# Normalised rows by one ScalarE operation of scale and bias, and a new step order on every engine

## The chip, the core and the metric

The kernel runs on one core of a Trainium2 chip. The core has a matrix engine (TensorE, PE; its weight loads are listed apart as PEld), a vector engine (VectorE, DVE), an activation engine (ScalarE, ACT), a general engine (GpSimd, POOL) and SyncE (SP), which here only issues DMAs. Each engine runs its own instruction list in order, and the lists meet only at semaphores. The metric is the device time of one execution in microseconds, the median of three.

## What is computed

One block of a transformer with adaptive layer norm over x of 8 batches x 1024 rows x 256 features, in fp32. The weights are 256x1024 and 1024x256.

```
h = layernorm(x) * (1 + ca) + sa              # ca, sa, ga, cb, sb, gb: one row of 256 per batch
x = x + ga * softmax((h*w_lhs) @ (h*w_rhs)^T) @ h
h = layernorm(x) * (1 + cb) + sb
x = x + gb * (relu(h @ W1 + b1) @ W2 + b2)
```

A layer norm is (x - mean) / sqrt(var + eps) over the 256 features of a row. Where products need more than the fast matmul format holds, an operand is split into a rounded part (`hi`) and a rest (`lo`), and three matmuls stand for one.

## The kernel before

Rows lie in tiles of 128 partitions, so a batch has 8 tiles in two halves (HT = 4). The work of a batch is cut into steps, and for each engine a table of text gives the order of the steps (`FIRST_STEPS` for batch 0, `SECOND_STEPS` for batch 1, `STEPS` for a loop over batches 2 to 6, `LAST_STEPS` for batch 7, `AFTER_STEPS` behind it). A suffix `-` means the step belongs to the batch before, `+` to the one after. So attention of batch b runs between the two feed-forward layers of batch b-1. `part` of each engine walks its table and emits the code of each step. Nothing else sets the order.

The steps that matter here, with n the tile or half:

- SC.n (PE: scores of a tile; DVE L864: copy to S with row maximum), ST and MX (DVE: stage blocks of S, row maxima of the lower half), MB.n (PE L655: maxima turned to columns), SB.n (DVE L887/L892: subtract the maximum), EX.n (ACT L793: exp), SM.n (ACT L806 rounded part `Phi`, DVE L911 rest `Plo`), AV.n (PE L690 to L694: attention times values; DVE L917 to L932: scale, add to x, statistics of the new row).
- L1.n: statistics of the next batch's rows (DVE L951/L954), and on POOL, in `statistics` (L1065), nm = -mean, var + eps and rs = 1/sqrt(var + eps). L2.n: the same for the rows behind attention.
- N1.n and N2.n: four row tiles of `ln_t` normalised as (x + nm) * rs, in `normalise` (L1074 to L1080) on POOL. Behind them stand BH.n and B2.n (DVE L990/L991: 32x32 transposes), a store and a load that complete the transpose (SP: SH/RH, S2/R2), and TH.n and T2.n (ACT and DVE: features scaled, shifted and split).
- VN.n (ACT L783): x + nm to `ln_v`, four tiles; VL.n (DVE L1038): times rs and the modulation row, four tiles; V.n (ACT L788, DVE L980): split into V.
- F.n (PE L593 to L595: a block of the first layer, six matmuls; ACT L715 relu and L719 rounded part; POOL L1088 the rest `hid_lo`), G.n (PE L530 to L536: second layer, twelve matmuls), OUT.n (DVE L1026/L1030: result times gb plus x), GT and OT (the last tiles), TP.0 (PE L662: transposes of batch 0's rows on PE).
- XG.n (DVE L1051), XC.n (POOL L1139): additions to x.

PE waits for: `scores_read`, `av_read`, `v_done` (V.n is split), `plo_done`, `hid_hi_done`, `hid_lo_done`, `col_read`, and at G.8 for `out_done`, since the accumulator of G.0 to G.7 must have been read by OUT.0.

Of the kernel before, what the change touches and what calls it, by code (L numbers as in the profile page):

```python
# [1170 lines left out]
```

## Time and profile before

| what | value |
|---|---|
| time, three executions | 693.47, 693.54, 694.78 us; median 693.54 us |
| profiled execution, first to last instruction (span) | 691.5 us |
| busy: PE, weight loads, DVE, ACT, POOL | 686.1, 627.7, 558.4, 427.5, 361.7 us |
| granted TensorE clock, mean | 1.00 of full speed |
| DMA: moved, mean rate | 77.54 MB, 112 GB/s |

The profile is one execution. It gives its span and no other time of its own: the median lies 2.0 us above the span, which is what lies around the first and the last instruction. Busy times of different engines overlap, so they don't add up to the span.

### The profile page before, as it was taken

Reading aid. Unit: us, or ns where it says so; the run is one execution under the profiler, and the core shown is the slowest. Engines: PE = TensorE matmul, PEld = TensorE weight load, DVE = VectorE, ACT = ScalarE, POOL = GpSimd, SP = SyncE. Lnnn points to the kernel's source line nnn. Section 1 sums busy time; section 2 is a strip of 40 time slices with the busy share of each in tenths; the row PEclk is TensorE's granted clock in tenths of the full one; section 3 lists DMA queues with packets and bytes.
Section 4 is the critical chain, followed back from the end, with each engine's and each line's share of the span. In section 5 each row is a group of like instructions: output and inputs, shape, how many; then the busy total and the mean of one; then the engine's idle time right before and its main releaser. Section 6 shows DMA issues by size and latency. Waiting matters only on the chain.

```text
span 691.5 us, 13488 instructions
## 1 busy us (share of the span) xinstructions
PE 686.1 (99%) x4621; PEld 627.7 (91%) x4621; DVE 558.4 (81%) x1059; ACT 427.5 (62%) x625; POOL 361.7 (52%) x396
## 2 busy tenths in 40 slices
PE   9999999999999999999999999999999999999998
PEld 8688899998999989998999989999899998999997
DVE  5699989799898898978989799887989887876421
ACT  3265398736786367683786647864678634845562
POOL 3572576636654386352872458643665434523644
PEclk9999999999999999999999999999999999999999
DMA  8211761137431382315622266112843126003300
GB/s 294 81 49 59 204 193 55 39 107 252 123 100 56 103 232 91 99 61 179 180 67 90 67 226 185 61 38 98 258 121 99 46 91 221 1 1 100 100 31 30
DMA packets 61663, 77.54 MB, mean 112 GB/s; under 512 B 5632, under 2 KB 54336, under 8 KB 61632
## 3 DMA queue, kind: packets, MB, share of 16 engines
q1 hardware_dynamic: 61632, 77.14, 35.5%
q8 instruction: 18, 0.29, 0.2%
q14 instruction: 13, 0.11, 0.1%
HBM read 46.15 MB, written 30.97 MB: 112 GB/s over the span
## 4 chain that ended last, share of the span: by engine, by line
PE 94%; DVE 4%; issue 0%; ACT 0%; DMA 0%; DVEq 0%; ACTq 0%; SPq 0%
PE col L595 9%; PE col L594 9%; PE col L593 9%; PE acc L530 8%; PE acc L531 8%; PE acc L536 8%; PE score L694 8%; PE score L690 8%; PE score L691 8%; PE score L578 4%; PE score L579 4%; PE score L580 4%; PE score L576 2%; PE score L584 2%; PE score L499 1%; DVE S L879 1%
## 5 line engine op out<-in xcount | busy, mean ns | idle before, releaser
L1088 POOL TENSOR_TENSOR hid_lo<-hid,hid_hi 128x512 fp32r<-128x512 f32 x127 | 175.4, 1386 | 143.2 <-ACT hid_hi L719 142.8
L715 ACT ACTIVATE hid<-col,b1T 128x512 f32<-128x512 f32 x128 | 87.0, 679 | 140.3 <-PE col L595 126.1
L530 PE MATMUL acc<-W2hi,hid_hi 128*128 128x256 f32 x480 | 119.2, 282 | 0.0
L531 PE MATMUL acc<-W2lo,hid_hi 128*128 128x256 f32 x480 | 116.9, 278 | 0.0
L690 PE MATMUL score<-V,Phi 128*128 128x258 f32 x448 | 108.8, 281 | 0.0
L691 PE MATMUL score<-V,Phi 128*128 128x256 f32 x448 | 108.6, 281 | 0.0
L719 ACT ACTIVATE hid_hi<-hid 128x512 fp32r<-128x512 f32 x128 | 81.0, 633 | 37.6 <-PE acc L536 29.8
L593 PE MATMUL col<-h2hi,W1hi 128*128 128x512 f32 x256 | 102.4, 400 | 0.0
L595 PE MATMUL col<-h2hi,W1lo 128*128 128x512 f32 x256 | 101.0, 395 | 0.0
L594 PE MATMUL col<-h2lo,W1hi 128*128 128x512 f32 x256 | 100.6, 393 | 0.0
L530 PEld LDWEIGHTS acc<-W2hi,hid_hi 128*128 128x128 f32 x480 | 90.4, 188 | 2.1
L531 PEld LDWEIGHTS acc<-W2lo,hid_hi 128*128 128x128 f32 x480 | 90.2, 188 | 1.8
L690 PEld LDWEIGHTS score<-V,Phi 128*128 128x128 f32 x448 | 85.0, 190 | 0.7
L691 PEld LDWEIGHTS score<-V,Phi 128*128 128x128 f32 x448 | 84.0, 188 | 0.6
L1069 POOL TENSOR_SCALAR nm<-mv 128x4 f32<-128x4 f32 x32 | 16.7, 523 | 129.2 <-DVE mv L932 104.2
L911 DVE TENSOR_TENSOR Plo<-S,Phi 128x1024 fp32r<-128x1024 f32 x56 | 70.2, 1269 | 8.1 <-ACT Phi L806 6.4
L536 PE MATMUL acc<-W2hi,hid_lo 128*128 128x256 f32 x480 | 76.6, 276 | 0.0
L864 DVE TENSOR_SCALAR_CACHE_REDUCE S<-score 128x1024 f32<-128x1024 f32 (+1 forms) x64 | 62.7, 980 | 15.2 <-PE score L584 12.9
L793 ACT ACTIVATE S<-S 128x1024 f32<-128x1024 f32 (+1 forms) x64 | 64.4, 1019 | 13.2 <-DVE S L879 7.7
L1139 POOL TENSOR_TENSOR x_cur<-x_cur,attn_mod 128x512 f32<-128x512 f32 x32 | 43.3, 1354 | 40.8 <-DVE ln_v L1038 40.8
L536 PEld LDWEIGHTS acc<-W2hi,hid_lo 128*128 128x128 f32 x480 | 64.6, 188 | 0.0
L694 PE MATMUL score<-V,Plo 128*128 128x258 f32 x448 | 62.8, 282 | 0.0
(139 smaller groups left out, 1493.2 us busy)
## 6 DMA issues: line engine op xcount, KB each, us to landing
block_rows<-blocks SPq DMA_DIRECT2D x29, 512.0 KB, 2.9
blocks<-block_rows SPq DMA_DIRECT2D x116, 128.0 KB, 3.0
x_cur<-x SPq DMA_DIRECT2D x16, 512.0 KB, 3.9
ln_t<-x SPq DMA_DIRECT2D x14, 512.0 KB, 4.8
score_blocks<-stage SPq DMA_DIRECT2D x14, 512.0 KB, 4.2
lower<-score_blocks SPq DMA_DIRECT2D x56, 128.0 KB, 2.9
out<-x_mlp SPq DMA_DIRECT2D x8, 512.0 KB, 3.0
out<-x_mlp SPq DMA_DIRECT2D x15, 256.0 KB, 2.2
```

What stands on the lines that cost most here:

```text
L530: nc.tensor.matmul(o, hi, W2hi[:, it, :], start=(it == 0 and (apart or t % 2 == 0)), stop=False, skip_group_check=True)
L531: nc.tensor.matmul(o, hi, W2lo[:, it, :], start=False, stop=False, skip_group_check=True)
L536: last = nc.tensor.matmul(o, lo, W2hi[:, it, :], start=False, stop=(it == FT - 1), skip_group_check=True)
L593: nc.tensor.matmul(col[n % 2][:], W1hi[:, kk, tile], h2hi[:, kk, cols], start=(kk == 0), stop=False)
L594: nc.tensor.matmul(col[n % 2][:], W1hi[:, kk, tile], h2lo[:, kk, cols], start=False, stop=False)
L595: last = nc.tensor.matmul(col[n % 2][:], W1lo[:, kk, tile], h2hi[:, kk, cols], start=False, stop=(kk == DK - 1))
L690: nc.tensor.matmul(o, Phi[:, slot, t, :], V[:, t, 0:VW], start=(t == 0), stop=False)
L691: nc.tensor.matmul(o[:, 0:D], Phi[:, slot, t, :], V[:, t, VP:VP + D], start=False, stop=False)
L694: last = nc.tensor.matmul(o, Plo[:, slot, t, :], V[:, t, VP:VP + VW], start=False, stop=(t == T - 1))
L715: nc.scalar.activation(hid[:, n % 2, :], col[n % 2][:], ACT.Relu, bias=b1T[:, n % FT:n % FT + 1]).then_inc(col_read, 1)
L719: nc.scalar.activation(hid_hi[:, n % RING, :], hid[:, n % 2, :], ACT.Copy).then_inc(hid_hi_done, 1)
L1088: G.tensor_tensor(hid_lo[:, n % RING, :], hid[:, n % 2, :], hid_hi[:, n % RING, :].bitcast(F32), ALU.subtract).then_inc(hid_lo_done, 1)
```

## The change

`normalise` on POOL is gone. N1 and N2 are steps of ACT now, each four activations that compute x * rs + nb, where nb = nm * rs is a new small operation at the end of `statistics` (with one more semaphore, `ln1_power` or `ln2_power`, between). VN computes x * rs + nb as well, so `ln_v` holds normalised rows, and VL on DVE is one tensor-tensor product with the modulation row over all four tiles, in place of four operations of two products. All tables of steps are new.

```diff
-        SC.6 SC.7 BH.0+ SB.2 VL.1 SM.0 MX.0 SB.3 V.1 L1.1+ SM.1 SB.4 OUT.0- AV.0 BH.1+ SB.5 AV.1 SM.2 SM.3
+        SC.7 BH.0+ VL.1 SB.1 SM.0 MX.0 SB.2 SB.3 L1.1+ OUT.0- SB.4 V.1 SM.1 SB.5 SM.2 BH.1+ AV.0 AV.1 AV.2
...
-                            nc.scalar.activation(ln_v[:, t, :], x_cur[:, i, :], ACT.Identity, bias=nm1[:, i:i + 1]).then_inc(v_mean, 1)
+                            nc.scalar.activation(ln_v[:, t, :], x_cur[:, i, :], ACT.Identity, scale=rs1[:, i:i + 1], bias=nb1[:, i:i + 1]).then_inc(v_mean, 1)
...
+                    elif kind == "N1":
+                        act.wait_ge(ln1_rstd, 2 * b + 3 + n)
+                        for t in range(HT):
+                            i = n * HT + t
+                            last = nc.scalar.activation(ln_t[:, t, :], ln_t[:, t, :], ACT.Identity, scale=rs1[:, i:i + 1], bias=nb1[:, i:i + 1])
+                        last.then_inc(ln1_done, 1)
+                    elif kind == "N2":
...
+                        act.wait_ge(ln2_rstd, 2 * batch + n + 1)
+                        for t in range(HT):
+                            i = n * HT + t
+                            last = nc.scalar.activation(ln_t[:, t, :], x_cur[:, i, :], ACT.Identity, scale=rs2[:, i:i + 1], bias=nb2[:, i:i + 1])
+                        last.then_inc(ln2_done, 1)
...
-                        for t in range(HT):
-                            i = n * HT + t
-                            dve.wait_ge(v_mean, HT * (2 * b + n - 2) + t + 1)
-                            V_.scalar_tensor_tensor(ln_v[:, t, :], ln_v[:, t, :], rs1[:, i:i + 1], attn_mod[:, 0, :], ALU.mult, ALU.mult).then_inc(v_ln, 1)
+                        dve.wait_ge(v_mean, HT * (2 * b + n - 2) + HT)
+                        V_.tensor_tensor(ln_v[:], ln_v[:], attn_mod[:, 0:1, :].broadcast_to([P, HT, D]), ALU.mult).then_inc(v_ln, HT)
...
-                G.tensor_tensor(rs[:, tiles], var_eps[:], half_power[:], ALU.pow).then_inc(rstd_done, 1)
-
-            def normalise(out_tiles, in_tiles, nm, rs, h, rstd_done, count, done):
-
-                wait_apart(pool, rstd_done, count)
-                for t in range(HT):
-                    i = h * HT + t
-                    last = G.tensor_scalar(out_tiles[:, t, :], in_tiles[:, t, :], nm[:, i:i + 1], rs[:, i:i + 1], ALU.add, ALU.mult)
-                last.then_inc(done, 1)
+                G.tensor_tensor(rs[:, tiles], var_eps[:], half_power[:], ALU.pow).then_inc(power_done, 1)
+                pool.wait_ge(power_done, count)
+                G.tensor_tensor(nb[:, tiles], nm[:, tiles], rs[:, tiles], ALU.mult).then_inc(rstd_done, 1)
```

Where the steps moved, at three places. DVE in the loop over batches 2 to 6, before: SB.3 (L889/L892) is followed by V.1 (L980) and the statistics of the next rows (L951).

```order
283 L903 TENSOR_TENSOR row_max<-row_max,left_max 128x4
284 L889 TENSOR_TENSOR S<-S,score 128x4x128
285 L892 TENSOR_TENSOR S<-lower,score 128x4x128
286 L980 TENSOR_TENSOR V<-ln_v,V 128x4x256
287 L364 ISA
288 L948 REGISTER_ALU
289 L951 BN_STATS stats<-ln_t 128x6 x4
```

The same engine and place of the change, from the first product of OUT.0 (L1050, L1054) on.

```order
292 L1054 TENSOR_TENSOR x_mlp<-acc,x_mlp 128x512
293 L1049 ISA
294 L1050 TENSOR_TENSOR acc<-acc,gb_all 128x512
295 L1053 REGISTER_ALU
296 L1054 TENSOR_TENSOR x_mlp<-acc,x_mlp 128x512
297 L911 TENSOR_TENSOR S<-S,score 128x8x128
298 L1004 TENSOR_TENSOR V<-ln_v,V 128x4x256
```

V.1 (L1004) now stands behind OUT.0 and SB.4 (L911), which waits for MB.1 of PE. On PE, MB.1 is followed by F.12, G.10 and AV.0 now; before, G.7 and then AV.0 followed it.

ACT in the same loop of the change: N1.1 (L815) and V.1 (L792) between F.10 (L719/L723) and EX.3 (L797).

```order
178 L719 ACTIVATE hid<-col,b1T 128x512
179 L720 REGISTER_ALU
180 L723 ACTIVATE hid_hi<-hid 128x512
181 L812 REGISTER_ALU
182 L815 ACTIVATE ln_t<-ln_t,nb,rs 128x256 x4
183 L790 REGISTER_ALU
184 L792 ACTIVATE V<-ln_v 128x4x256
185 L796 REGISTER_ALU
186 L797 ACTIVATE S<-S 128x8x128
```

ACT in that place before: V.1 (L788) came earlier, between F.8 and F.9 (L715/L719).

```order
160 L715 ACTIVATE hid<-col,b1T 128x512
161 L716 REGISTER_ALU
162 L719 ACTIVATE hid_hi<-hid 128x512
163 L786 REGISTER_ALU
164 L788 ACTIVATE V<-ln_v 128x4x256
165 L715 ACTIVATE hid<-col,b1T 128x512
```

So four activations came in, in front of a V.1 that itself stands two F steps later.

POOL at the end of the program, before: the last L2.1 (L1069 to L1072) and N2.1 (L1079) stand ahead of the last feed-forward blocks.

```order
146 L1069 TENSOR_SCALAR nm<-mv 128x4
147 L1070 TENSOR_SCALAR var_eps<-mv 128x4
148 L1072 TENSOR_TENSOR rs<-var_eps,half_power 128x4
149 L1079 TENSOR_SCALAR ln_t<-x_cur,nm,rs 128x256 x4
150 L1088 TENSOR_TENSOR hid_lo<-hid,hid_hi 128x512 x15
```

The same of the change.

```order
143 L1091 TENSOR_SCALAR nm<-mv 128x4
144 L1092 TENSOR_SCALAR var_eps<-mv 128x4
145 L1094 TENSOR_TENSOR rs<-var_eps,half_power 128x4
146 L1096 TENSOR_TENSOR nb<-nm,rs 128x4
147 L1104 TENSOR_TENSOR hid_lo<-hid,hid_hi 128x512 x15
```

N2.1 has left POOL; on ACT it stands behind the first two F steps of `AFTER_STEPS`. The AV.7 of batch 7, on whose rows it works, was followed by G.12, F.15 and G.13 to G.15 on PE and is now PE's last step of batch 7.

## Rows read from the trace of the kernel before

**Rows 1.** The page: engine shares, and the shares of the chain that ended last.

```profile
PE 686.1 (99%) x4621; PEld 627.7 (91%) x4621; DVE 558.4 (81%) x1059; ACT 427.5 (62%) x625; POOL 361.7 (52%) x396
...
PE 94%; DVE 4%; issue 0%; ACT 0%; DMA 0%; DVEq 0%; ACTq 0%; SPq 0%
```

**Rows 2.** Busy us by stage: window, its us, PE, PEld, DVE, ACT, POOL, clock, DMA.

```profile
0.00:17.39 17.39, 15.81 (x112) 14.50 (x113) 8.86 (x31) 5.35 (x10) 5.85 (x16) 1.00 0.87 295
17.39:67.64 50.25, 49.92 (x231) 38.52 (x232) 42.96 (x103) 23.37 (x32) 26.58 (x33) 1.00 0.20 64
67.64:150.61 82.97, 82.85 (x571) 76.44 (x571) 73.41 (x139) 54.81 (x81) 47.15 (x48) 1.00 0.41 121
...
315.08:397.32 82.24, 82.24 (x572) 76.36 (x571) 71.52 (x132) 54.68 (x80) 44.63 (x48) 1.00 0.38 121
...
644.01:688.13 44.12, 44.10 (x290) 39.97 (x288) 12.97 (x18) 23.62 (x36) 23.71 (x23) 1.00 0.16 51
688.13:691.50 3.37, 0.00 (x0) 0.00 (x0) 0.85 (x2) 0.00 (x0) 0.59 (x1) 0.98 0.46 156
```

**Rows 3.** The waits of PE: total us, times, longest.

```profile
PE score L683 <- DVE x_cur L926: 0.3, 1, 0.3
```

**Rows 4.** Groups of instructions: line, engine, shapes, count | busy us, mean ns.

```profile
L1079 POOL TENSOR_SCALAR ln_t<-x_cur,nm,rs 128x256 f32<-128x256 f32 x64 | 37.8, 606 | 3.4 <-POOL rs L1072 2.3 <-issue 1.0
L1072 POOL TENSOR_TENSOR rs<-var_eps,half_power 128x4 f32<-128x4 f32 x32 | 35.6, 1112 | 2.7
L1079 POOL TENSOR_SCALAR ln_t<-ln_t,nm,rs 128x256 f32<-128x256 f32 x56 | 31.4, 577 | 1.5 <-POOL rs L1072 1.5
L1038 DVE SCALAR_TENSOR_TENSOR ln_v<-ln_v,rs,attn_mod 128x256 f32<-128x256 f32 x56 | 24.5, 498 | 0.5 <-ACT ln_v L783 0.4
L736 ACT ACTIVATE featT<-blocks,mod_b 128x512 f32<-128x512 f32 x30 | 24.2, 807 | 16.0 <-DMA blocks<-block_rows 11.2 <-DVE Rlo L999 4.8
L783 ACT ACTIVATE ln_v<-x_cur,nm 128x256 f32<-128x256 f32 x56 | 23.7, 495 | 0.7 <-DMA x_cur<-x 0.7
L745 ACT ACTIVATE h2hi<-featT 128x512 fp32r<-128x512 f32 x32 | 20.2, 633 | 1.0
L1070 POOL TENSOR_SCALAR var_eps<-mv 128x4 f32<-128x4 f32 x32 | 9.5, 297 | 2.2
```

**Rows 5.** In time order: batch 7's G.7 and two F steps, and OUT.0 on DVE.

```profile
667.33 0.28 PE L530 MATMUL acc<-W2hi,hid_hi 128*128 128x256 f32 x1
...
668.34 0.70 DVE L1026 TENSOR_TENSOR acc<-acc,gb_all 128x512 f32<-128x512 f32 x1 [7.53 <-PE acc L536]
...
668.72 0.39 PE L593 MATMUL col<-h2hi,W1hi 128*128 128x512 f32 x1
...
670.09 0.39 PE L593 MATMUL col<-h2hi,W1hi 128*128 128x512 f32 x1
...
670.40 0.69 DVE L1030 TENSOR_TENSOR x_mlp<-acc,x_mlp 128x512 f32<-128x512 f32 x1
```

**Rows 6.** Batch 7's MB.1 and SB.4 in time order, and the line of V.n.

```profile
604.30 0.60 PE L655 MATMUL score<-ident,row_max 128*128 128x128 f32 x4
...
604.93 1.22 DVE L887 TENSOR_TENSOR S<-S,score 128x1024 f32<-128x1024 f32 x1 [1.00 <-PE score L655]
...
L980 DVE TENSOR_TENSOR V<-ln_v,V x14: 1211/1474/1660, 84.4 to 598.9; 128x1024 fp32r<-128x1024 f32 x14
```

**Rows 7.** Batch 0: TP.0 on PE, and the read of AV.7 on DVE.

```profile
63.07 1.04 PE L662 MATMUL score<-ident,ln_t 128*128 128x128 f32 x8
...
68.91 0.42 DVE L926 TENSOR_TENSOR x_cur<-score,x_cur 128x256 f32<-128x256 f32 x1
```

**Rows 8.** The last rows' chain: N2.1 (POOL), T2.1 (ACT, DVE).

```profile
644.55 2.18 POOL L1079 TENSOR_SCALAR ln_t<-x_cur,nm,rs 128x256 f32<-128x256 f32 x4 [0.21 <-issue]
...
657.24 0.80 ACT L736 ACTIVATE featT<-blocks,mod_b 128x512 f32<-128x512 f32 x1
...
660.11 0.69 DVE L1002 TENSOR_TENSOR h2lo<-featT,h2hi 128x512 fp32r<-128x512 f32 x1 [0.68 <-ACT h2hi L745]
```

More of the change, by code:

```diff
@@ L80 @@
+        N2.0 TH.1+ EX.7 F.14- SM.7 F.15- T2.0
     """,
     "dve": """
-        SC.0 ST.0 SC.1 B2.1- XG.2- XG.3- SC.2 ST.1 VL.0 ST.2 L1.0+ V.0 SC.3 ST.3 VL.1 SC.4 SB.0 BH.0+ SB.1
-        SB.2 SC.5 T2.1- V.1 SC.6 L1.1+ SC.7 SM.0 MX.0 SM.1 SB.3 AV.0 OUT.0- SB.4 BH.1+ SM.2 AV.1 SB.5 SB.6
-        SM.3 AV.2 AV.3 SM.4 SB.7 XG.0 TH.0+ SM.5 B2.0 XG.1 AV.4 SM.6 AV.5 SM.7 AV.6 TH.1+ AV.7 T2.0 OUT.1-
+        SC.0 ST.0 B2.1- XG.2- SC.1 XG.3- SC.2 ST.1 VL.0 ST.2 V.0 SC.3 ST.3 L1.0+ VL.1 SC.4 SB.0 SC.5 SB.1
@@ L85 @@
+        BH.0+ V.1 T2.1- SC.6 SB.2 SC.7 SM.0 SB.3 MX.0 L1.1+ SB.4 OUT.0- SM.1 SB.5 AV.0 SM.2 BH.1+ AV.1 SM.3
+        SB.6 AV.2 SM.4 TH.0+ AV.3 SB.7 SM.5 XG.0 XG.1 SM.6 AV.4 AV.5 B2.0 TH.1+ AV.6 SM.7 AV.7 OUT.1- T2.0
     """,
     "pool": """
-        N2.1- F.0- XC.0 F.1- F.2- L1.0+ N1.0+ F.3- XC.1 F.4- F.5- F.6- F.7- L1.1+ XC.2 N1.1+ F.8- F.9- XC.3
-        F.10- F.11- F.12- L2.0 N2.0 F.13- F.14- F.15- L2.1
+        F.0- XC.0 F.1- F.2- F.3- L1.0+ F.4- XC.1 XC.2 F.5- F.6- F.7- XC.3 F.8- L1.1+ F.9- F.10- F.11- F.12-
@@ L806, in part @@
                         nc.scalar.activation(Phi[:, n % RING, :, :], S[:, :, n * P:(n + 1) * P], ACT.Copy).then_inc(phi_done, 1)
+                    elif kind == "N1":
[5 more added lines that the diff above has]
+                    elif kind == "N2":
+                        batch = b if n == 0 else f
+                        if n == 1:
+                            act.wait_ge(blocks_done, ph.turn_base(b))
+                        elif "next" in ph.has:
+                            act.wait_ge(blocks_done, ph.turn(b, "TH", 1) + 1)
+                        else:
+                            act.wait_ge(blocks_done, ph.turn(b, "T2", 1) + 1)
+                        act.wait_ge(ln2_rstd, 2 * batch + n + 1)
[3 more added lines that the diff above has]
+                        last.then_inc(ln2_done, 1)
             over_batches(act, part)
@@ L1117, in part @@
                             last.then_inc(w_ready, 1)
-                    elif kind == "N1":
-                        normalise(ln_t, ln_t, nm1, rs1, n, ln1_rstd, 2 * b + 3 + n, ln1_done)
-                    elif kind == "N2":
-                        batch = b if n == 0 else f
-                        if n == 1:
-                            pool.wait_ge(blocks_done, ph.turn_base(b))
-                        elif "next" in ph.has:
-                            pool.wait_ge(blocks_done, ph.turn(b, "TH", 1) + 1)
-                        else:
-                            pool.wait_ge(blocks_done, ph.turn(b, "T2", 1) + 1)
-                        normalise(ln_t, x_cur[:, n * HT:(n + 1) * HT, :], nm2, rs2, n, ln2_rstd, 2 * batch + n + 1, ln2_done)
                     elif kind == "XC":
```

98 lines of the change are left out of this document (51 added, 47 removed).

## The prediction, made before the changed kernel had run

> **What bounds the kernel now.** I read the engine shares first, then the stretches, then the waits of PE. PE is busy 686.1 of 691.5 us, and 94% of the chain that ended last is PE's [rows 1]. A busy share alone may hide short waits, so the stretches decide: batches 2 to 6 take 82.24 us each and PE is busy for all of it [rows 2]. What PE leaves idle is before its work starts (17.39 - 15.81 = 1.6 us), behind its last matmul (3.37 us) and in batches 0 and 1: 0.33 us in the first, and 0.73 us by which the second is longer than a middle one [rows 2]. PE has one wait of 0.3 us in its list [rows 3]. So the reader should see a kernel in which any change of ACT, DVE or POOL is worth nothing unless it makes PE wait, or takes away one of these small remainders. PE's matmuls are the same ones in the change, in another order.
>
> By the Trainium skill (Perfetto Trace Analysis, "Identifying the Most-Contended Engine"), matmul busy time is a bad measure and the busy share of weight loads a good one. That share is 76.36 of 82.24 us in a middle batch [rows 2], so by that rule up to 5.9 us a batch would be open to a better order, 41 us over the five, and the time about 652 us.
>
> I don't follow it: two starts of an F step (six matmuls of 512 columns) lie 670.09 - 668.72 = 1.37 us apart [rows 5], 0.23 us a matmul, in stretches where nothing is waited for, so loads idle there by the length of the matmul and an order can't change that.
>
> **The change part by part.**
>
> *Work taken and added.* POOL loses 120 tile operations, 37.8 + 31.4 = 69.2 us [rows 4], and gains 32 small ones, nb. The trace has none of that kind; between 0.30 (L1070, same width, one input) and 1.11 us (L1072, two inputs, a power) [rows 4] I take 0.3, so 10 us. POOL comes to about 302 us of 691. None of this is on PE's path.
>
> ACT gains the same 120 tiles, 16 a middle batch. An activation with no operand by row takes 633 ns and one with both scale and bias by row 807 ns, at 512 elements [rows 4]: 174 ns for two. VN has one and takes 495 ns at 256 elements [rows 4]. With the second it lies between 495 and 495 + 174 = 669 ns; I take 582, half of the 174 for each. A middle batch gets 16 x 0.582 + 8 x 0.087 = 10.0 us more, so ACT has 64.7 us of 82.24 where it had 54.7 [rows 2]. It fits, if it stands in the right places.
>
> DVE loses four operations of 498 ns in each VL, 2.0 us, and gets one of 1024 elements. Nearest are V.n's 1211 to 1660 ns [rows 6], so it gains 0.3 to 0.8 us a half. DVE is busy 71.5 of 82.24 us [rows 2] and PE doesn't wait for it: nothing.
>
> *Middle batches, G.8.* With the new PE order G.7, F.10, F.11, G.8, the wait for `out_done` comes close. From G.7's first matmul at 667.33 OUT.0 starts after 1.01 us (668.34, when half of G.7 is done) and ends at 670.40 + 0.69 = 671.09, 3.76 us after G.7 began [rows 5]. G.8 begins one G and two F later: 1.39 + 2 x 1.37 = 4.13 us [rows 5]. So 0.37 us are left if DVE is free when G.7's first half is done, and it costs nothing; before, two AV steps stood in between as well. Hidden by: F.10 and F.11.
>
> *Middle batches, AV.0.* On DVE V.1 now waits behind SB.4, which waits for MB.1, and AV.0 of PE waits for V.1. SB.4 starts 0.63 us after MB.1 (604.93 against 604.30) and takes 1.22 us; V.1 takes 1.21 to 1.66 us [rows 6]. So V.1 ends 3.06 to 3.51 us after MB.1 began. AV.0 comes behind MB.1 (an estimate: it shows 0.60 us until its last transpose has drained, and some 0.25 us of that overlap the next step; that is 0.35 us), F.12 and G.10: 0.35 + 1.37 + 1.39 = 3.11 us [rows 5, 6]. The stall is 0 to 0.4 us in each of five batches. I take V.1 at its shortest, since POOL, whose subtractions it can meet, has nothing to do there: F.10's rest is done by then, and F.11's comes after TH.0. Sum 0.0, bound 5 x 0.4 = 2.0 us. On ACT N1.1 (4 x 0.58 = 2.3 us) now stands in front of V.1, behind F.10. F.10 is released 3 x 1.37 = 4.1 us ahead of MB.1 (F.11, G.8 and G.9 stand between) and DVE gets to V.1 1.85 us after MB.1, so ACT has 4.1 + 1.85 = 5.9 us for F.10 (two activations, 1.3), N1.1 (2.3) and V.1 (1024 elements, at most twice the 633 ns: 1.3) [rows 4]: hidden with 1.0 us to spare.
>
> *Batch 0 into 1.* TP.0 (at 63.07, about 0.9 of its 1.04 us until the next matmul) moves behind AV.7, so the read of AV.7, which let the second half of batch 1's SC.0 go on at 68.91 + 0.42 = 69.33 [rows 7], gets that much cover. But TH.1 on DVE, for which SC.0's first half waits, now stands behind AV.6's read. Bounds: the whole 0.73 us by which batch 1 is longer won [rows 2], or 0.4 us lost, one operation of the read (0.42) [rows 7]. I take 0.1 lost, since a read is more than one such operation, and so longer than the cover. The small operation nb also delays batch 0's first normalisation by 0.3 us, but PE's transposes of these rows come after modulation matmuls, and in the second half DVE is still busy with the first: nothing.
>
> *Behind batch 7.* AV.7 is PE's last step of batch 7, so L2.1 and N2.1 start later. N2.1 began at 644.55, 0.54 us after the stretch began, and T2.1's last split ended at 660.11 + 0.69 = 660.80, 16.8 us into it [rows 8]. Now N2.1 stands behind F.1 on ACT: two F on PE (2.74), two activations of 0.63 [rows 4, 5], so from 4.0 on, and 4 x 0.58 us later, at 6.3, it is done, where it was done at 2.7 (644.55 + 2.18). L2.1 with nb (0.3 + 0.3 + 1.1 + 0.3 = 2.0 us [rows 4]) is ready by then if AV.7's read took under 2 us. T2.1's end moves by 0 to 3.6 us, to 16.8 to 20.4: on ACT it began at 657.24 with no idle time ahead of it [rows 8], so it waited for ACT and not for its load, and takes only a part of the delay; I take two thirds, 19.2. F.8 begins after F.0 to F.7 and G.0 to G.5, fourteen steps of 1.37 us, at 19.2. A race with no margin: 0 to 1.2 us. I take 0.
>
> *The sum* against the profiled span: 691.5 + 0.1 = 691.6 us; with the 2.0 us by which the median lay above it, 693.6 us.
>
> **The rivals.**
>
> *DVE comes late to OUT.0 or V.1 (slower).* DVE has 71.5 us of work in 82.24, and its order has waits for PE in it, behind which the rest of the list queues. From 0.37 us of lateness at OUT.0 on, G.8 stalls PE, and from a V.1 over 1.3 us on, AV.0 does. For it: both margins are smaller than anything that PE met before, where it waited once. Against: DVE loses 0.6 to 1.6 us of work a batch ahead of that place. At 0.4 us in each of six batches: 693.6 + 2.4 = 696.0 us. Chance 0.16.
>
> *A lock between POOL and DVE.* V.1 takes 1.21 us or up to 1.66 [rows 6], so something shares a path with it. If a POOL subtraction began just before V.1, and V.1 then waited for all of it, V.1 would end a whole 1.3 us late: five times 1.2 us, 699.6 us. That is the rule of the Trainium skill (SBUF — State Buffer, "SBUF: two separate sides"), by which the pair of ports that DVE and GpSimd share is held for a whole instruction. The 0.45 us between V.n's shortest and longest show a part of it at most. Chance 0.03.
>
> *ACT falls behind (slower).* The new activations take not 0.58 but over 0.83 us each, or meet a wait, and N1.1 uses up the 1.0 us in front of V.1. At 669 ns, the upper bound, it is 0.35 us and nothing happens. With 1.4 us of slip: 0.4 x 5 = 2.0, 695.6 us. Chance 0.03.
>
> *The remainders go (faster).* The 0.33 and 0.73 us of batches 0 and 1 and a part of the 1.6 us at the start: 693.5 - 1.5 = 692.0 us. Chance 0.05. That weight loads tell the truth and the new order packs PE closer gets 0.01.
>
> *It doesn't do what it says*: the normalisation doesn't get shorter at all (577 and 606 ns on POOL, some 582 on ACT). That seems likely to me, and gives the forecast's time.
>
> **How the numbers follow.** Forecast 0.72, with its own range 692.8 to 694.6. The range for 8 in 10 reaches into the remainders' case below and past 696.0 above: 692.4 to 696.5. About 0.2%, 1.4 us, is what a measurement of this kernel can tell from no change. Faster by more needs the remainders or the packing: 0.06. Slower by more: 0.16 + 0.03 + 0.03 = 0.22. Within: 0.72.
>
> **What would show it.** Right: middle batches of 82.24 us with PE busy throughout; activations L815 and L829 near 582 ns; no wait of G.8 or AV.0 over 0.1 us. Wrong: a middle batch over 82.5 us, with idle time of PE or of its weight loads before L534 (G) or L694 (AV), released by DVE; F.8 behind batch 7 waiting for T2.1; a batch 1 other than 82.9 us. If the time moves and the middle batches don't, my ends are wrong, not the argument.

## The result, and the profile after

The changed kernel takes 695.78 us (median of 8 executions, 695.42 to 696.45), the kernel before 693.5 us (8 executions beside them). The ratio is 1.0032, with a 95% interval of 1.0021 to 1.0042: 2.3 us slower. The forecast was 693.6 us and no change. Its own range, 692.8 to 694.6 us, missed the time; the wide one, 692.4 to 696.5 us, holds it.

The page of the changed kernel shows what was expected of the engines: POOL falls from 361.7 to 300.8 us (302 was forecast), ACT rises from 427.5 to 492.6, and PE stays the bound, as in [rows 1].

```profile
span 694.1 us, 13451 instructions
PE 688.4 (99%) x4621; PEld 628.1 (90%) x4621; DVE 546.2 (79%) x1017; ACT 492.6 (71%) x745; POOL 300.8 (43%) x308
PE 96%; DVE 3%; issue 0%; ACT 0%; POOL 0%; DMA 0%; DVEq 0%; POOLq 0%; SPq 0%
```

Busy time by stage answers to [rows 2] (window, its us, PE, PEld, DVE, ACT, POOL, clock, DMA): batch 0, batch 1, batch 2, batch 3, batch 6, batch 7, and what comes behind.

```profile
17.23:68.43 51.20, 50.42 (x233) 38.33 (x231) 42.75 (x105) 27.41 (x42) 19.63 (x24) 1.00 0.20 64
68.43:151.36 82.93, 82.92 (x571) 76.23 (x572) 70.18 (x134) 65.08 (x99) 36.92 (x39) 1.00 0.42 122
151.36:233.73 82.37, 82.37 (x573) 76.50 (x572) 69.28 (x126) 63.87 (x98) 35.85 (x34) 1.00 0.39 122
233.73:316.31 82.58, 82.58 (x573) 76.46 (x572) 69.81 (x127) 63.48 (x97) 36.55 (x36) 1.00 0.41 121
481.54:564.15 82.61, 82.61 (x573) 76.46 (x572) 69.81 (x127) 63.49 (x97) 36.55 (x36) 1.00 0.40 121
564.15:646.42 82.27, 82.27 (x573) 76.23 (x572) 65.18 (x100) 51.67 (x76) 32.33 (x28) 1.00 0.26 81
646.42:690.80 44.38, 44.31 (x290) 40.09 (x288) 9.93 (x20) 25.47 (x40) 23.10 (x22) 1.00 0.14 45
```

Batch 0 is 0.95 us longer, batch 2 by 0.13, batches 3 to 6 by 0.36 on average (0.34, 0.33, 0.42 and 0.37), batch 7 by 0.06; batch 1 is 0.04 shorter. The eight sum to 629.2 us against 626.6: 2.6 us, as much as the spans differ by.

Of batch 0's 0.95 us only 0.73 are a loss. The changed row begins it with MF.2, the old one with SC.0, which waits for ACT's `L_first`. So the changed kernel begins it 0.22 us sooner, 1.72 us after the first matmul of the step before it and not 1.94. That is a small gain, but it is counted here as length of batch 0. The line of PEld's list for that wait in the kernel before, which the changed kernel's list doesn't have:

```profile
PEld score L576 <- ACT L_first L771: 0.9, 1, 0.9
```

From that common matmul to batch 1, the kernel before takes 52.19 us, the changed one 52.91 and first_old (below) 52.34. Behind batch 7 the changed kernel loses 0.2 us more, so the spans come to differ by 2.6 us too.

PE counts as busy for the whole of each middle batch all the same. So the wait hides inside matmuls whose modelled ends overlap it, and PE's list of waits (the answer to [rows 3]) names only places of the start and of batches 0 and 1. The list of the weight loads shows it. Three of the five lines of PE's list, then two of PEld's of the changed kernel, then PEld's line for the same code in the kernel before.

```profile
PE score L503 <- POOL ident L1084: 1.5, 1, 1.5
PE score L687 <- DVE x_cur L950: 0.2, 1, 0.2
PE score L666 <- ACT ln_t L829: 0.2, 1, 0.2
```
```profile
PEld score L588 <- issue: 2.0, 8, 0.3
PEld score L588 <- DVE S L888: 1.9, 7, 0.3
```
```profile
PEld score L584 <- DVE S L864: 0.4, 2, 0.2
```

L588 transposes a block of S in SC.1, and S comes from DVE's copy of SC.0 (L888). To see where in a batch PE loses time, I took each PE step's start to the next step's start and compared it with the same step of the kernel before. In batches 3 to 6 two places stand out: SC.1 takes 2.67 to 2.71 us and not 2.45, and AV.5 and AV.6 take 0.05 and 0.10 us more. Batch 2 loses at AV.5 and AV.6 alone. The stretch around SC.1 of batch 6, in time order: TH.1 (L1021, L1023), the first operation of OUT.1, T2.0 (L1026) and the copy (L888) on DVE; then the transpose and the next matmul on PE.

```profile
476.80 1.54 DVE L1021 SCALAR_TENSOR_TENSOR Llo<-featT,wl,Lhi 128x512 fp32r<-128x512 f32 x1
478.26 0.74 DVE L1023 SCALAR_TENSOR_TENSOR Rlo<-featT,wr,Rhi 128x512 fp32r<-128x512 f32 x1
...
481.63 0.67 DVE L1050 TENSOR_TENSOR acc<-acc,gb_all 128x512 f32<-128x512 f32 x1
...
484.27 1.28 DVE L1026 TENSOR_TENSOR h2lo<-featT,h2hi 128x512 fp32r<-128x512 f32 x2
485.48 1.22 DVE L888 TENSOR_SCALAR_CACHE_REDUCE S<-score 128x1024 f32<-128x1024 f32 x1
```
```profile
486.76 0.33 PE L588 MATMUL score<-ident,S 128*128 128x128 f32 x1
486.99 0.50 PE L597 MATMUL col<-h2hi,W1hi 128*128 128x512 f32 x1
```

The copy ends at 486.70, the transpose begins at 486.76. Before, F.0 stood between SC.0 and SC.1 on PE and gave the copy 1.37 us of cover. The copy isn't later than before: it ends 5.15 us after SC.0 began (481.54), and ended 5.45 us after it before. But PE comes to the transpose 1.37 us sooner now, and so whatever delays DVE counts. DVE has no gap from TH.1 to the copy, and TH.1's first operation takes 1.54 us, its second 0.74.

The new operations have the sizes that were estimated (the answer to [rows 4]); nb is cheap:

```profile
L829 ACT ACTIVATE ln_t<-x_cur,nb,rs 128x256 f32<-128x256 f32 x64 | 33.3, 592 | 28.9 <-POOL nb L1096 28.7
L787 ACT ACTIVATE ln_v<-x_cur,nb,rs 128x256 f32<-128x256 f32 x56 | 29.0, 589 | 6.9 <-DVE V L1004 6.9
L815 ACT ACTIVATE ln_t<-ln_t,nb,rs 128x256 f32<-128x256 f32 x56 | 28.9, 587 | 9.8 <-POOL nb L1096 9.8
L1096 POOL TENSOR_TENSOR nb<-nm,rs 128x4 f32<-128x4 f32 x32 | 7.0, 219 | 2.5
```

### The profile page after: what moved, and what is told of

It is laid out like the page before. It is cut to its first block, busy times and chain, and to the rows that moved or that the text cites. A ratio compares the mean times of both kernels' runs of the same rounds, so it can differ in the third digit from the quotient of the medians.

```text
span 694.1 us, 13451 instructions
## 1 busy us (share of the span) xinstructions
PE 688.4 (99%) x4621; PEld 628.1 (90%) x4621; DVE 546.2 (79%) x1017; ACT 492.6 (71%) x745; POOL 300.8 (43%) x308
## 4 chain that ended last, share of the span: by engine, by line
PE 96%; DVE 3%; issue 0%; ACT 0%; POOL 0%; DMA 0%; DVEq 0%; POOLq 0%; SPq 0%
PE col L597 9%; PE col L599 9%; PE col L598 9%; PE acc L534 8%; PE acc L535 8%; PE acc L540 8%; PE score L694 8%; PE score L698 8%; PE score L695 8%; PE score L582 5%; PE score L583 4%; PE score L584 4%; PE score L580 2%; PE score L588 2%; PE score L503 1%; PE score L659 1%
## 5 line engine op out<-in xcount | busy, mean ns | idle before, releaser
L1104 POOL TENSOR_TENSOR hid_lo<-hid,hid_hi 128x512 fp32r<-128x512 f32 x127 | 180.7, 1427 | 205.4 <-ACT hid_hi L723 205.2
L719 ACT ACTIVATE hid<-col,b1T 128x512 f32<-128x512 f32 x128 | 86.8, 678 | 69.4 <-PE col L599 59.0
L534 PE MATMUL acc<-W2hi,hid_hi 128*128 128x256 f32 x480 | 117.6, 279 | 0.0
L694 PE MATMUL score<-V,Phi 128*128 128x258 f32 x448 | 109.3, 282 | 0.0
L723 ACT ACTIVATE hid_hi<-hid 128x512 fp32r<-128x512 f32 x128 | 81.0, 633 | 17.0 <-PE acc L540 10.4
L534 PEld LDWEIGHTS acc<-W2hi,hid_hi 128*128 128x128 f32 x480 | 90.4, 188 | 2.1
L694 PEld LDWEIGHTS score<-V,Phi 128*128 128x128 f32 x448 | 85.0, 190 | 1.0
L888 DVE TENSOR_SCALAR_CACHE_REDUCE S<-score 128x1024 f32<-128x1024 f32 (+1 forms) x64 | 62.4, 981 | 29.8 <-PE score L584 19.2
L935 DVE TENSOR_TENSOR Plo<-S,Phi 128x1024 fp32r<-128x1024 f32 x56 | 71.9, 1295 | 3.1 <-ACT Phi L810 2.4
L797 ACT ACTIVATE S<-S 128x1024 f32<-128x1024 f32 (+1 forms) x64 | 64.8, 1021 | 13.1 <-DVE S L903 6.4
L582 PE MATMUL score<-Rhi,Lhi 128*128 128x512 f32 (+2 forms) x168 | 59.5, 354 | 0.2 <-DVE Rlo L1023 0.2
```

The source lines that it names most:

```text
L534: nc.tensor.matmul(o, hi, W2hi[:, it, :], start=(it == 0 and (apart or t % 2 == 0)), stop=False, skip_group_check=True)
L582: nc.tensor.matmul(o, Lhi[:, kk, tile], Rhi[:, kk, cols], start=(kk == 0), stop=False)
L694: nc.tensor.matmul(o, Phi[:, slot, t, :], V[:, t, 0:VW], start=(t == 0), stop=False)
L719: nc.scalar.activation(hid[:, n % 2, :], col[n % 2][:], ACT.Relu, bias=b1T[:, n % FT:n % FT + 1]).then_inc(col_read, 1)
L1104: G.tensor_tensor(hid_lo[:, n % RING, :], hid[:, n % 2, :], hid_hi[:, n % RING, :].bitcast(F32), ALU.subtract).then_inc(hid_lo_done, 1)
```

## The experiments

Batch lengths are read as above, from the start of PE's first step of a batch (MF.2 or SC.0 in batch 0) to the next batch's first step. They are more exact than the times: batch 0's start itself lies between 17.1 and 18.4 us in these fourteen profiles, in kernels with the same first steps too (17.23 in the changed kernel, 18.27 in f15_split). The sum is that of batches 0 to 7; a ratio is to the kernel before, run beside it. Between a kernel whose batch 0 begins with SC.0 (before, ops_only, both act_move, first_old, both_fixes, first_split) and one that begins it with MF.2, 0.22 us of batch 0 and of the sum are the earlier start and no loss.

| kernel | time, us | ratio, 95% interval | batch 0 | batches 3 to 6, mean | sum |
|---|---|---|---|---|---|
| before | 693.5 | | 50.25 | 82.24 | 626.6 |
| changed | 695.78 | 1.0032, 1.0021 to 1.0042 | 51.20 | 82.60 | 629.2 |
| ops_only | 693.76 | 1.0003, 0.9994 to 1.0012 | 50.19 | 82.24 | 626.5 |
| order_only | 699.78 | 1.0089, 1.0074 to 1.0103 | 51.43 | 82.71 | 631.0 |
| t2_first | 696.91 | 1.0046, 1.0033 to 1.0060 | 51.18 | 82.64 | 629.8 |
| first_old | 695.51 | 1.0028, 1.0017 to 1.0038 | 50.40 | 82.60 | 628.3 |
| act_move | 716.52 | 1.0327, 1.0311 to 1.0342 | 52.17 | 85.59 | 645.9 |
| act_move3 | 735.45 | 1.0593, 1.0567 to 1.0618 | 53.81 | 90.22 | 669.1 |
| sc1_cover | 695.62 | 1.0027, 1.0015 to 1.0038 | 51.19 | 82.35 | 628.7 |
| sm6_first | 698.35 | 1.0065, 1.0051 to 1.0079 | 51.21 | 82.98 | 631.4 |
| f15_short | 695.23 | 1.0019, 1.0010 to 1.0028 | 51.22 | 82.38 | 628.5 |
| both_fixes | 695.75 | 1.0021, 1.0012 to 1.0030 | 50.42 | 82.36 | 628.2 |
| f15_split | 695.88 | 1.0025, 1.0016 to 1.0034 | 51.20 | 82.38 | 628.7 |
| first_split | 695.17 | 1.0015, 1.0006 to 1.0024 | 50.40 | 82.41 | 627.9 |

**Operations or order.** Two kernels split the change. ops_only has nb, the two-operand VN and the one-operation VL with all tables of before and N1, N2 on POOL. order_only has the new tables with the old operations, N1 and N2 on POOL behind their statistics.

```diff
 ops_only, POOL of STEPS (as before)
+        N2.1- XC.0 F.0- XC.1 F.1- F.2- L1.0+ F.3- N1.0+ F.4- F.5- F.6- XC.2 F.7- F.8- F.9- L1.1+ N1.1+ F.10-
 order_only, POOL of SECOND_STEPS
+        N2.1- F.0- XC.0 F.1- F.2- F.3- L1.0+ N1.0+ F.4- XC.1 XC.2 F.5- F.6- F.7- XC.3 F.8- L1.1+ N1.1+ F.9-
```

> The new operations of VN, VL and of the statistics (with nb) in the old step orders; N1 and N2 stay on GpSimd as (x + nm) * rs. Theory 1 (the 2.3 us come from single short waits of PE that the new order makes): no change from the kernel before, 693.5 us within 0.4, middle batches of 82.24 us, batch 0 50.25 us. Theory 2 (the new operations themselves slow what feeds PE, in any order): a good part of the 2.3 us is here, over 694.5 us, with middle batches over 82.3 us.

> The new step orders with the old operations: N1 and N2 back on GpSimd, each right behind its statistics (N2.1 at the head of the list), VN and VL as before. Theory 1: batches 3 to 6 still lose about 0.25 us each at SC.1 (its transposes wait for VectorE, where SC.0 stands behind OUT.1 and T2.0); the waits at TP.0 and AV.4 of batch 0 and of AV.6 for SM.6, which hang on N1.1 and N2.0 on ScalarE, go, so 694.5 to 695.2 us. Theory 2: 693.5 us.

ops_only takes the time of before, and a middle batch the same 82.24 us:

```profile
315.48:397.72 82.24, 82.24 (x572) 76.36 (x571) 70.97 (x126) 55.51 (x80) 45.34 (x52) 1.00 0.39 121
```

order_only missed what was expected of it: it is slower than the changed kernel, by 1.9 us in the sum and by 1.8 behind batch 7 (G.0 there takes 1.3 us too long, waiting for POOL's `hid_lo`). At SC.1 it loses more than the changed kernel (0.36 to 0.40 us in batches 3 to 6), but nothing at AV.5 and AV.6 (0.07 at AV.7): what is lost there belongs to N2.0 on ACT. Batch 7 is 1.0 us longer than before, half of it at SC.1, half ahead of AV.0. So most of the cost is the order's, the three operations of ops_only cost nothing, and the move to ACT costs at one place and gives more back at others. The place of N1 and N2 on POOL in the new order is one choice of several, so order_only isn't the new order alone.

```profile
PE acc L536 <- POOL hid_lo L1088: 1.0, 1, 1.0
PE score L578 <- DVE Rlo L999: 0.6, 1, 0.6
```

**The move to ACT without the new orders.** act_move has the changed kernel's operations, the tables of before, and N1 and N2 as ACT steps in them. act_move3 puts them at other places of ACT's row in the loop alone, N2.0 and, on DVE, B2.0 behind SM.6.

```diff
 STEPS, ACT: act_move against before
-        F.0- VN.0 F.1- V.0 F.2- T2.1- F.3- VN.1 F.4- EX.0 L1.0+ SM.0 F.5- EX.1 F.6- F.7- EX.2 F.8- V.1 F.9-
+        N2.1- F.0- VN.0 F.1- V.0 F.2- T2.1- F.3- VN.1 F.4- EX.0 L1.0+ SM.0 F.5- N1.0+ EX.1 F.6- F.7- EX.2 F.8-
 STEPS, ACT: act_move3 against act_move
-        V.1 F.9- EX.3 SM.1 F.10- N1.1+ TH.0+ SM.2 SM.3 F.11- EX.4 EX.5 SM.4 F.12- SM.5 F.13- TH.1+ F.14- N2.0
+        V.1 F.9- EX.3 SM.1 F.10- SM.2 N1.1+ SM.3 TH.0+ F.11- EX.4 EX.5 SM.4 F.12- SM.5 F.13- TH.1+ F.14- EX.6
```

> The new operations with the step orders of before, but with N1 and N2 on ACT, put where ACT has room in the old order (N2.1- first, N1.0+ behind F.5-, N1.1+ behind F.10-, N2.0 behind F.14- in a middle batch). It is the change without its new orders, POOL relieved of 69 us. Theory A (the move to ACT is itself harmless, as ACT has 17 us a middle batch to spare, and the 0.3 us a batch come from the places that the new DVE and PE orders give SC.0's copy and SM.6): middle batches 82.24 us as in ops_only, time 693.3 to 694.2 us. Theory B (ACT is too full for 16 more operations in any order: exp, Phi and relu come late by what stands ahead of them): middle batches 82.6 us or more, with PE waits released by ACT (hid_hi, Phi) of 0.2 us and over, time 695.5 us or more.

> act_move with another place for the new ACT steps in the loop of batches 2 to 6 alone: N1.1+ behind SM.2 and TH.0+ behind SM.3 (in act_move both stood ahead of SM.2, and ACT waited 2.5 us for POOL in front of N1.1+), and N2.0 behind SM.6 with B2.0 behind SM.6 on DVE (in act_move N2.0 stood ahead of EX.6). PE and POOL keep the order of before. If the 3.0 to 3.8 us a batch that act_move lost are the places of these steps on ACT and not ACT's load, most of AV.2's 1.1 us and of the 0.7 to 0.9 us at F.14 and G.12 goes, and batches 3 to 6 come to 82.3 to 83.7 us, time 701 to 709 us (batches 0 and 1 stay as they were, together with their start 5 us behind the kernel before). If ACT's load is the cause, the batches stay at 85 us and the time at 714 us or more.

Both forecasts of a harmless move fell: 3.4 us a batch are lost in act_move and 8 in act_move3. By the signs set down beforehand that spoke for ACT's load. But the load can't be the cause by itself, since it is 63.5 us of work a batch in the changed kernel too, which takes 82.6 us. Batch 5 of act_move, batch 5 of act_move3:

```profile
410.25:495.54 85.29, 83.27 (x573) 76.42 (x572) 71.64 (x127) 63.49 (x96) 37.58 (x36) 1.00 0.39 117
```
```profile
419.72:508.58 88.86, 84.44 (x573) 77.51 (x571) 70.55 (x126) 63.39 (x97) 36.07 (x36) 0.98 0.38 112
```

What differs is what stands behind a wait. In act_move ACT waits for POOL's statistics in front of N1.1+, with TH.0+ and SM.2 behind it:

```profile
455.75 2.08 ACT L815 ACTIVATE ln_t<-ln_t,nb,rs 128x256 f32<-128x256 f32 x4 [2.51 <-POOL nb L1096]
```

BH.1+ on DVE waits for TH.0+ in turn (1.4 us), with AV.1's read and SM.2 behind it, and AV.2 takes 1.1 us more. In act_move3 the wait for POOL is behind SM.2, but TH.0+ comes later still: BH.1+ waits 2.4 us, and AV.2 takes 2.0 us more. And B2.0 on DVE comes late, with it T2.0, and AV.7's read stands behind T2.0 in the old DVE row, so that the next batch's SC.0 waits. The largest line of PE's waits in act_move3:

```profile
PE score L582 <- DVE x_cur L952: 11.5, 4, 3.6
```

So of the orders that were tried only the new ones carry the move: two placements in the old order cost 22.5 and 41.9 us of time, the new tables 2.3. Part of the 41.9 us is the clock's (last section). A third placement, act_move2, with TH.0+ behind EX.5 and SM.4 on ACT, can't run at all: BH.1+ on DVE waits for TH.0+, and EX.5 waits for SB.5, which stands behind BH.1+ on DVE. Whether a better placement in the old order exists is open.

**Batch 0.** first_old puts batch 0 back into its old rows (TP.0 stays behind AV.7; N1.0+, N1.1+ and N2.0 stand on ACT).

```diff
 FIRST_STEPS, ACT: first_old against the changed kernel
-        WS.0 N1.0+ EU.0 MC.0 L1.0+ EU.1 EX.0 EX.1 EU.2 EU.3 EX.2 EX.3 TH.0+ N1.1+ EX.4 EX.5 EX.6 EX.7 TH.1+
+        WS.0 N1.0+ EU.0 EU.1 EU.2 EX.0 EX.1 EU.3 EX.2 L1.0+ TH.0+ EX.3 N1.1+ EX.4 EX.5 EX.6 TH.1+ MC.0 EX.7 N2.0
...
```

> The changed kernel with batch 0 in its old order: N1.0, N1.1 and N2.0 on ScalarE put in behind WS.0, EX.3 and EX.7, TP.0 left behind AV.7. Theory 1: the four waits of batch 0 (at AV.4, AV.7, TP.0 and SC.0 of batch 1) go, batch 1 starts at 67.5 us in place of 68.4, and the time falls by 0.9 us to 694.9 us. Rival (batch 0 is longer since ScalarE now has the normalisations at all): batch 1 still starts at 68.2 us or later.

Batch 0 takes 50.40 us and not 51.20, the rest is unchanged. 0.6 of these 0.8 us are won; the other 0.2 are the earlier start that MF.2 gave, which is given up again. Batch 1 begins at 68.14 us, where 67.5 was expected and the rival said 68.2 or later. By its lengths the rival is out, though batch 0 is still 0.15 us longer than before. The time, expected at 694.9 us, came to 695.51 and moved less than its uncertainty.

**SC.1's wait.** t2_first moves T2.0 ahead of OUT.1- at the end of DVE's row. sc1_cover does that too and puts F.0- between SC.0 and SC.1 on PE in batches 2 to 7, as it was before in batches 2 to 6. One row of each table is shown; steps that seem missing stand in the row next to it.

```diff
 STEPS, DVE: both
...
-        SM.3 SM.4 TH.0+ AV.3 XG.0 SM.5 SB.6 SB.7 AV.4 B2.0 XG.1 SM.6 AV.5 SM.7 AV.6 TH.1+ AV.7 OUT.1- T2.0
+        TH.0+ AV.3 XG.0 SM.5 SB.6 SB.7 AV.4 B2.0 XG.1 SM.6 AV.5 SM.7 AV.6 TH.1+ AV.7 T2.0 OUT.1-
 STEPS, PE: sc1_cover
-        SC.0 SC.1 F.0- SC.2 SC.3 F.1- F.2- G.0- SC.4 F.3- SC.5 MB.0 G.1- F.4- F.5- SC.6 SC.7 F.6- G.2- G.3-
+        SC.0 F.0- SC.1 SC.2 SC.3 F.1- F.2- G.0- SC.4 F.3- SC.5 MB.0 G.1- F.4- F.5- SC.6 SC.7 F.6- G.2- G.3- F.7-
```

> The changed kernel with one edit: on VectorE, T2.0 stands ahead of OUT.1 at the end of batches 1 to 6. Theory 1: VectorE gets to SC.0's copy earlier or T2.0 no longer adds its 1.2 us behind OUT.1, SC.1 goes back from 2.67 to 2.70 us to 2.46 us, batches 3 to 6 take 82.35 us in place of 82.6, and the time falls by 0.9 us to 694.9 us. If OUT.1's own start sets it (it waits for G.15), SC.1 stays and nothing changes: 695.8 us.

> The changed kernel with T2.0 ahead of OUT.1- on DVE (as in t2_first) and, on PE, F.0- between SC.0 and SC.1 in batches 2 to 7, so that the copy of SC.0 gets 1.37 us of cover, as before. Theory C (SC.1 runs 0.22 to 0.28 us long because its closing transpose meets SC.0's copy on DVE, which is late by OUT.1 and T2.0, and nothing else): the 0.25 us go in each of batches 2 to 7, batches 3 to 6 come to 82.35 to 82.45 us, time 695.4 us (t2_first less 1.5). Rival D (DVE is late there by a fixed amount and the wait moves to SC.2 or SC.3, or F.0 waits for T2.0): middle batches stay at 82.6 us, time 696.5 to 697.0 us.

The swap alone does nothing (SC.1 is still 0.25 to 0.29 us too long), as both steps stand ahead of the copy in either order; that miss was mine to see beforehand. With F.0 as cover the wait is gone: batches 3 to 6 take 82.35 us, and batch 6's copy has long ended when the transpose begins.

```profile
485.91 1.21 DVE L888 TENSOR_SCALAR_CACHE_REDUCE S<-score 128x1024 f32<-128x1024 f32 x1
```
```profile
488.49 0.27 PE L588 MATMUL score<-ident,S 128*128 128x128 f32 x1
```

The time came to 695.62 us (695.4 was expected). Batch 2 is longer in these two kernels than in the changed one (82.9 us against 82.4): some matmuls in 182 to 197 us start 0.1 us late there with no releaser named. That stays open.

**AV.5 and AV.6.** sm6_first puts EX.6 and SM.6 ahead of N2.0 on ACT, and SM.6 ahead of B2.0 on DVE, in the loop.

```diff
 STEPS, ACT
...
-        SM.6 EX.7 MC.0 SM.7 F.14- F.15- T2.0
+        N2.0 EX.7 MC.0 SM.7 F.14- F.15- T2.0
 STEPS, DVE
...
-        SM.3 SM.4 TH.0+ AV.3 XG.0 SM.5 SB.6 SB.7 AV.4 B2.0 XG.1 SM.6 AV.5 SM.7 AV.6 TH.1+ AV.7 OUT.1- T2.0
+        TH.0+ AV.3 XG.0 SM.5 SB.6 SB.7 AV.4 SM.6 B2.0 XG.1 AV.5 SM.7 AV.6 TH.1+ AV.7 OUT.1- T2.0
```

> The changed kernel, in the loop of batches 2 to 6 with EX.6 and SM.6 ahead of N2.0 on ACT, and SM.6 directly behind AV.4 on DVE. Theory A: AV.5 and AV.6 run 0.05 and 0.10 us long because SM.6 stands behind N2.0, which waits for POOL's L2.0; the 0.15 us go in each of five batches: batches 82.4 to 82.5 us, time 694.9 to 695.2 us. If instead B2.0, which comes 1.6 us later, delays T2.0 so that OUT.1, T2.0 and SC.0's copy come later on DVE, SC.1's wait grows by as much as is won: 695.7 us or more.

Both halves came. AV.5 and AV.6 lose nothing any more, and batch 2, which has no other loss, takes 82.21 us. But N2.0, T2.0 and with them SC.0's copy come later (the copy ends 5.71 us after SC.0 began and not 5.15), so SC.1 is 0.78 us too long. Batch 2 and batch 6:

```profile
151.71:233.92 82.21, 82.21 (x573) 76.44 (x572) 68.81 (x125) 62.73 (x96) 36.62 (x34) 1.00 0.39 122
482.84:565.84 83.00, 82.59 (x572) 76.41 (x571) 69.76 (x127) 63.57 (x97) 37.33 (x36) 1.00 0.39 120
```

**Why DVE is late: TH.1 beside F.15.** In f15_short POOL's subtraction of F.15 covers 64 of 512 columns. f15_split leaves nothing out and makes it in four pieces of 128 columns; first_split has these pieces in first_old.

```diff
 POOL, kind F: f15_split
-                        G.tensor_tensor(hid_lo[:, n % RING, :], hid[:, n % 2, :], hid_hi[:, n % RING, :].bitcast(F32),
-                                        ALU.subtract).then_inc(hid_lo_done, 1)
+                        pieces = 4 if n == NF - 1 else 1
+                        w = HR // pieces
+                        for c in range(0, HR, w):
+                            last = G.tensor_tensor(hid_lo[:, n % RING, c:c + w], hid[:, n % 2, c:c + w],
+                                                   hid_hi[:, n % RING, c:c + w].bitcast(F32), ALU.subtract)
+                        last.then_inc(hid_lo_done, 1)
```

> The changed kernel in which POOL's subtraction of F.15 covers 64 of 512 columns (the rest of hid_lo keeps what an earlier block left there), so that it lasts under 0.4 us and not 1.3. It lies beside TH.1 on DVE at the end of a middle batch. Theory E (TH.1's four operations take 3.76 us and not some 2.9 because they share a path to memory with that subtraction, and that makes OUT.1, T2.0 and SC.0's copy late): TH.1 ends 0.3 us or more earlier, SC.1's 0.22 to 0.25 us in batches 3 to 6 fall to under 0.1, time 694.9 to 695.2 us. Rival F (OUT.1 is late by its place behind AV.7's read, which PE sets, and TH.1 has slack): SC.1 stays 0.2 us long and the time at 695.6 to 696.0 us.

> The changed kernel in which POOL makes F.15's subtraction in four pieces of 128 columns one behind the other, all 512 columns as before and nothing left out. In the changed kernel's trace every DVE operation with two inputs that began while a POOL operation ran lasted longer by that operation's remaining time less 0.13 to 0.20 us (TH.1's first: 1.54 us where 0.75 is usual, with 0.99 left of POOL's 1.28). Theory G (a DVE operation of this kind is held until the POOL instruction in progress has ended, and no longer): with pieces of 0.32 us it is held 0.3 us at most, TH.1's first operation lasts 0.75 to 1.05 us, the pieces behind it wait for DVE in turn, SC.1's 0.22 us go in batches 3 to 6, which come to 82.4 us, and the time to 695.0 to 695.5 us. Rival H (the two share bandwidth, or DVE is held until POOL is idle): TH.1's first operation stays at 1.3 us or over, and batches 3 to 6 at 82.55 us or over. Rival I: the four pieces let DVE in between, F.15's rest comes so late that G.15's matmuls or SC.0 wait for it: a new PE wait released by POOL.

> first_old (batch 0 in its old order) with the same four pieces for F.15's subtraction. It is the version that gives back most of what the changed kernel lost while it keeps its order in all other batches. If the two add: batch 0 at 50.40 us, batches 3 to 6 at 82.4 us; the sum over batches 0 to 7 falls from 629.2 us (the changed kernel's) by 0.8 + 4 x 0.2 = 1.6 to 627.6 us, against 626.6 us of the kernel before; time 694.1 to 694.7 us, ratio about 1.001. It isn't expected to beat the kernel before, since AV.5 and AV.6 keep their 0.15 us a batch.

L1021's durations (min/median/max) in the changed kernel, in f15_short and in f15_split:

```profile
L1021 DVE SCALAR_TENSOR_TENSOR Llo<-featT,wl,Lhi x28: 709/746/1544, 59.4 to 561.5; 128x512 fp32r<-128x512 f32 x28
```
```profile
L1021 DVE SCALAR_TENSOR_TENSOR Llo<-featT,wl,Lhi x28: 710/747/753, 59.9 to 560.7; 128x512 fp32r<-128x512 f32 x28
```
```profile
L1021 DVE SCALAR_TENSOR_TENSOR Llo<-featT,wl,Lhi x28: 710/745/945, 60.4 to 561.4; 128x512 fp32r<-128x512 f32 x28
```

With a short F.15, TH.1 takes 2.74 us from start to end instead of 3.53 and SC.1 waits no more: batches 3 to 6 take 82.38 us. With pieces, TH.1's later operations take 0.94 to 0.95 us each, SC.1's wait goes as well, and the batches take 82.38 us. So the holding lasts as long as POOL's instruction in progress, and DVE and POOL then take turns. The pieces are held too and last 0.9 us where a free one takes 0.46. TH.1 as a whole is only 0.17 us shorter (3.36 us), which is just enough for SC.1. The times don't say as much: f15_split's 695.88 us missed the 695.0 to 695.5 expected, and why the 0.2 us a batch don't show in them is open. Starts of batch 0 scatter by more than a microsecond, as said above.

**Together.** both_fixes joins the rows of first_old and sc1_cover.

> The changed kernel with the two edits that won time apart put together: batch 0 in its old order (first_old) and T2.0 ahead of OUT.1- with F.0- between SC.0 and SC.1 in batches 2 to 7 (sc1_cover). If batch 0's and the loop's losses are separate, they add: batch 0 at 50.40 us, batches 3 to 6 at 82.35 us, batch 7 at 82.15 us, span 693.1 to 693.4 us and time 694.4 to 694.9 us; what is left against the kernel before is the 0.1 us of AV.6 in five batches and some 0.5 us of batch 2. If they are not separate (the order of batch 0 hands its wait on to batch 1), the time stays at 695.3 us or over. In no case faster than the kernel before by more than can be measured.

In the batches the two add: 50.42 and 82.36 us. Of the sum 1.0 us goes (0.8 won beyond the earlier start of MF.2 that is given up), not all that was hoped for, as batch 1 (83.21) and batch 7 (82.53) came out longer. In batch 1, SC.1 takes 2.67 to 2.69 us in first_old, first_split and both_fixes and 2.48 in those that keep the changed batch 0, so some 0.2 us of batch 0's wait are handed on, as the rival had it. SC.5 of batch 1 takes 1.09 to 1.51 us from profile to profile where the steps are the same; I can't put a cause to that. In batch 7 0.3 us are lost ahead of AV.0, which waits for V.1 on DVE; why V.1 is late in this profile is open. The time was expected at 694.4 to 694.9 and came out at 695.75, though the kernel before, too, stood 0.7 us higher there. first_split has the lowest ratio of the changed family: 1.0015 (1.0006 to 1.0024), 1.3 us of the sum back (1.0 without the earlier start), and still behind the kernel before. Its time was expected at 694.1 to 694.7 us and came to 695.17. No version is faster than the kernel before, and none was expected to be.

## Why the prediction was right or wrong

- **The bound and the sizes** were right. PE bounds the kernel, the activation takes 587 to 592 ns (582 forecast), the normalisation isn't shorter than on POOL, POOL's total is 300.8 us (302). The operations that ops_only has cost nothing. One sum was wrong: 5.9 us a batch are 29 us over five batches, not 41, so the time by that rule would have been about 664 us and not 652. No run here came near either.
- **That the time lies in the wide range is luck.** That range reached up to 696.5 us for DVE coming late to OUT.0 or V.1, which did not happen. What came was a loss of the same size at places that the prediction gave nothing.
- **G.8 and AV.0** held with margins close to those forecast. In batch 6 G.7 began at 520.04, OUT.0 ended at 523.71 and G.8 began at 524.18: 0.47 us left (0.37 forecast). V.1 ended on DVE at 529.92 and AV.0 began at 530.13: 0.21 us (0.05 forecast). Batches 2 to 5 show the same two margins. The answer to [rows 5, 6]: DVE did not come late to these, so that rival did not happen.
- **The step that failed** is the one on middle batches: it named two places where PE could wait and gave the others nothing. The change also took F.0 from between SC.0 and SC.1, and put N2.0 on ACT ahead of EX.6 and SM.6. Those make SC.1 0.22 to 0.26 us longer in four batches and AV.5 and AV.6 0.15 us in five: 1.7 us, of which sc1_cover and sm6_first each remove their own part. SC.1 needs both causes, the missing cover and POOL's hold on TH.1: without the hold, the same order loses nothing there (f15_short). (T2.0 behind OUT.1- on DVE, the third thing that changed there, costs nothing: t2_first.)
- **The rival of a lock between POOL and DVE** was given 0.03, and its mechanism is there, at another place. I had looked at V.n alone [rows 6] and took 0.45 us for "a part of it at most". That was a misreading: V.n never met a whole POOL operation. In the kernel before, the V.n shown here began with 0.39 us left of POOL's operation and lasted 0.26 us longer than the shortest:

```profile
187.75 1.30 POOL L1088 TENSOR_TENSOR hid_lo<-hid,hid_hi 128x512 fp32r<-128x512 f32 x1 [1.36 <-ACT hid_hi L719]
188.66 1.47 DVE L980 TENSOR_TENSOR V<-ln_v,V 128x1024 fp32r<-128x1024 f32 x1 [2.31 <-ACT V L788]
```

  The line that TH.0 and TH.1 issue shows a longer hold there, of 1.04 us. It is the first operation of TH.0, once in each of batches 2 to 6, and PE didn't wait for it:

```profile
L997 DVE SCALAR_TENSOR_TENSOR Llo<-featT,wl,Lhi x28: 719/746/1786, 55.7 to 553.2; 128x512 fp32r<-128x512 f32 x28
```

- **Batch 0 into 1** was bounded at 0.73 us won to 0.4 lost; batches 0 and 1 together lost 0.91, or 0.69 without the earlier start of batch 0 (which is a part of the rival "the remainders go" that did happen). The bounds looked at the seam alone. Most of it is inside batch 0, where `nb` and the N steps were said to cost nothing: N1.1+ stands ahead of EX.4 on ACT (AV.4 waits 0.2), TH.0 ahead of AV.5's read on DVE (AV.7 waits 0.2), N2.0 behind TH.1 (TP.0 waits 0.2), TH.1 behind AV.6's read (SC.0 waits 0.2), and AV.7's read adds the rest. first_old takes 0.6 us of it back.
- **Behind batch 7** the race was called right: T2.1 ended 18.9 us after that stretch began (19.2 forecast), F.8 began at 19.4, with 0.5 us to spare. The whole end is 0.2 us longer, where nothing was forecast.
- **What was to show it right or wrong** was half good: "a middle batch over 82.5 us" came true, and idle time of the weight loads released by DVE did too, but ahead of L588 (SC.1) and not of L534 or L694, where I would have looked. In PE's own rows it doesn't show, as the wait lies under modelled matmul ends.

## What to carry to other kernels

When PE is full and the order of steps is changed, compare the new row of PE step by step with everything that each step waits for, not only at the places with the smallest known margin; a step that once stood between a producer and its reader was cover. When work moves to another engine, its price is not its duration but what is queued behind the wait in front of it: with the same 63.5 us of ACT work a batch the kernel lost 2.3, 22.5 or 41.9 us here. And before an order is judged, read the minimum and the maximum of each repeated DVE line: where the maximum was twice the median here, a POOL operation lay beside it.
